# Layer 1's attention heads: the last two chunks of the value weighing move into the next head, with two accumulator banks

## The reference

```python
q = (hidden_states @ Wq.T + bq) * scaling          # 128 x 256, 16 heads of 16
k = key_value_states @ Wk.T + bk                   # 12544 x 256
v = key_value_states @ Wv.T + bv
scores = jnp.einsum('bhtd,bhsd->bhts', q, k) + bias
probs = jax.nn.softmax(scores, axis=-1)
attn = jnp.einsum('bhts,bhsd->bhtd', probs, v)
...
return attn @ Wo.T + bo
```

## Time and profile before

| | |
|---|---|
| median of 3 runs | 3257.34 us (3256.66, 3257.34, 3260.52) |
| profiled execution | 3260.9 us, its span 3259.2 us |
| mean granted TensorE clock | 0.968 |
| PE matmul busy | 3022.2 us (93%) |
| DVE busy | 1473.0 us (45%) |
| ACT busy | 1469.7 us (45%) |
| DMA, whole span | 577.84 MB, mean 177 GB/s |

### The profile page before, as it was taken

The page is one execution under the profiler, slowest core; times in us unless marked ns, Lnnn a source line. Parts: engine busy times, 40 slices in busy tenths (PEclk is TensorE's granted clock), DMA queues, the critical chain, the costliest instruction groups (busy, mean ns, idle before and its releaser), DMA issues. The chain is left out here.

```text
span 3259.2 us, 65496 instructions
## 1 busy us (share of the span) xinstructions
PE 3022.2 (93%) x23319; PEld 1909.9 (59%) x23319; DVE 1473.0 (45%) x4096; ACT 1469.7 (45%) x2522; POOL 230.1 (7%) x177
## 2 busy tenths in 40 slices
PE   8999999998797999998799999999999988999988
PEld 5555555556484666664455555555555675666678
DVE  3223232321526777765333333333333325888632
ACT  2332333333314788883244444444444432565621
POOL 2332313130000000000000000000000000000000
PEclk9999999999897999998999999999999987999979
DMA  6878787878249999965311111111111255656455
GB/s 222 285 259 255 252 253 253 253 241 277 96 144 365 363 363 373 359 258 188 136 40 59 40 59 40 59 59 40 59 55 44 78 167 152 153 148 154 117 185 188
DMA packets 301309, 577.84 MB, mean 177 GB/s; under 512 B 75569, under 2 KB 247425, under 8 KB 289921
## 3 DMA queue, kind: packets, MB, share of 16 engines
q1 hardware_dynamic: 301209, 576.58, 52.6%
HBM read 395.49 MB, written 181.05 MB: 177 GB/s over the span
## 5 line engine op out<-in xcount | busy, mean ns | idle before, releaser
L1762 DVE TENSOR_SCALAR_CACHE_REDUCE all_S<-l2x_scores 128x448 f32<-128x448 f32 x448 | 261.0, 620 | 413.9 <-PE l2x_scores L1678 413.9
L1826 ACT COPY early_nat_in<-l2x_key_bank 128x448 f32<-128x448 f32 x224 | 119.2, 532 | 485.1 <-PE l2x_key_bank L1665 483.7
L1665 PE MATMUL l2x_key_bank<-ahead_ctx,early_nat_out 128*64 128x448 f32 x1536 | 331.0, 552 | 0.0
L648 PE MATMUL prep_work<-prep_wv,prep_ctxT 128*128 128x512 f32 x688 | 300.3, 594 | 0.1
L1034 DVE CUSTOM_DVE_ANT_0 all_S<-l1x_scores,l1x_bias 128x448 f32<-128x448 f32 x448 | 261.7, 621 | 79.3 <-PE l1x_scores L946 70.4
L1270 DVE TENSOR_REDUCE l3x_rowmax<-l3x_scores 128x1 f32<-128x448 f32 x448 | 263.6, 622 | 39.5 <-PE l3x_scores L1190 38.0
L1345 ACT ACTIVATE l3x_pT<-l3x_turned 128x896 f32<-128x896 f32 x224 | 204.9, 917 | 164.4 <-PE l3x_turned L1198 161.3
L1701 PEld LDWEIGHTS l2x_out<-l2x_pT,l2x_v_half 128*64 128x64 f32 x3136 | 203.4, 137 | 96.8 <-issue 96.6
L1101 ACT ACTIVATE all_S<-all_S,l1x_negmax 128x896 f32<-128x896 f32 x224 | 232.8, 1042 | 50.4 <-DVE l1x_negmax L1047 34.5
L1841 ACT ACTIVATE all_S<-all_S,l2x_negmax 128x896 f32<-128x896 f32 x224 | 233.6, 1044 | 25.2 <-DVE l2x_total L1780 23.8
L1678 PE MATMUL l2x_scores<-early_nat_in,early_nat_out 64*128 64x448 f32 x896 | 229.1, 588 | 8.9 <-ACT early_nat_in L1826 8.2
(11 more groups left out here) (650 smaller groups left out, 4151.4 us busy)
## 6 DMA issues: line engine op xcount, KB each, us to landing
l1x_bias<-in_fside_Bx16xSxS_dram SPq DMA_DIRECT2D x112, 896.0 KB, 6.8
scratch_k<-prep_kparts SPq DMA_DIRECT2D x84, 672.0 KB, 3.3
l1x_k_half<-scratch_k SPq DMA_DIRECT2D x32, 1568.0 KB, 9.9
l2x_v_half<-scratch_v SPq DMA_DIRECT2D x32, 1568.0 KB, 6.3
keys_k<-scratch_k SPq DMA_DIRECT2D x32, 1176.0 KB, 7.3
scratch_k<-prep_kparts SPq DMA_DIRECT2D x56, 448.0 KB, 4.9
scratch_v<-prep_st_v SPq DMA_DIRECT2D x11, 2048.0 KB, 9.3
scratch_v<-prep_st_v SPq DMA_DIRECT2D x14, 1536.0 KB, 7.2
```

The lines of the kernel that those rows point to most:

```text
L648: last = nc.tensor.matmul(w[:, h, :], ctxT[:, k, j * P:(j + 1) * P], wv2[:, k, h * 512:(h + 1) * 512], start=(k == 0), stop=(k == KT - 1))
L1665: last = nc.tensor.matmul(keys_ps[half * VW:(half + 1) * VW, 0:HB], wk_cur[:, k, :], ahead.piece[c // 2][:, k, cols], start=(k == 0), stop ...
L1762: nc.vector.tensor_scalar(com.S[:, b * HB:(b + 1) * HB], scores_ps[half][:, 0:HB], 1.0, -3.4e38, ALU.mult, ALU.max, accum_out=rowmax[:, b: ...
```

## The change

`head_stream` is split: it keeps the one head of L0, in the same sequence, and a new `head_stream_biased` takes L1's sixteen. In it

- PE weighs chunks 9, 10 and 11 behind the last scores (chunk 8 still beside them). Chunks 12 and 13 are weighed in chunks 0 and 1 of the next head, behind its scores; `sum_tiles` follows in chunk 3. The last head weighs all its own.
- two accumulator banks take turns by the head's parity: the old `out` bank and `last_ps`, the bank that the projections use before and after. The product of `sum_tiles` goes beside the accumulators in the same bank. A head's first weighing waits for the division two heads back.
- DVE does `sum_of` at the head's end; `leave_bank` (copy of the bank, reciprocal) behind the scores of chunk 2 of the next head and `divide` behind those of chunk 4.
- PE's and DVE's loops have seven turns of two heads; heads 0 and 15 are written out.
- SP loads the second half of a head's values behind bias 1 of the head's own stretch and the first half of the next head's behind bias 5.
- DVE clears two banks at the start, behind a wait for `q_ready`.

```diff
-    def tensor_head(pe, h, following):
-        for c in range(GRP + lag):
-            if c < GRP:
-                turn(pe, h, c)
-                if following:
-                    scores(pe, h + 1, c)
+    def tensor_head(pe, h, odd, first=False, following=True):
+        for c in range(GRP):
+            turn(pe, h, c)
+            if following:
+                scores(pe, h + 1, c)
             if c >= lag:
-                weigh(pe, h, c - lag)
-        if tiles > 1:
-            sum_tiles(pe, h)
+                weigh(pe, h, odd, c - lag)
+            elif c < left and not first:
+                weigh(pe, h - 1, 1 - odd, GRP - left + c)
+            if c == left + 1 and not first:
+                sum_tiles(pe, h - 1, 1 - odd)
+        for c in range(GRP - lag, GRP - left if following else GRP):
+            weigh(pe, h, odd, c)
...
+        tensor_head(pe, 0, 0, first=True)
+        with pe.Fori(0, HEADS // 2 - 1) as i:
+            tensor_head(pe, i * 2 + 1, 1)
+            tensor_head(pe, i * 2 + 2, 0)
+        tensor_head(pe, HEADS - 1, 1, following=False)
+        sum_tiles(pe, HEADS - 1, 1)
...
+    def sum_of(dve, h):
         dve.wait_ge(exp_done, h * GRP + GRP)
         nc.vector.reduce_sum(total[:, :], rowsum[:, :], AX).then_inc(rowsum_taken, 1)
+
+    def leave_bank(dve, h, odd):
+        dve.wait_ge(weighed, h * GRP + GRP + ring)
+        nc.vector.tensor_copy(out_parts[:, :], banks[odd][:, 0:P]).then_inc(parts_ready, 1)
         dve.wait_ge(rowsum_taken, h + 2)
         nc.vector.reciprocal(inverse[:, :], total[:, :]).then_inc(out_step, 1)
+
+    def divide(dve, h, odd):
         dve.wait_ge(out_step, h + 1)
-        dve.wait_ge(weighed, h * GRP + GRP + ring)
...
+        dve.wait_ge(summed, h + 1)
+        nc.vector.tensor_scalar(att[:, bass.ds(h * VW, VW)], banks[odd][:, P:P + VW], inverse[:, 0:1], None,
                                 ALU.mult).then_inc(out_taken, 1)
...
-    def vector_head(dve, h, following):
+    def vector_head(dve, h, odd, first=False, following=True):
         for c in range(GRP):
             if by[c] == "v":
                 copy_turned(dve, nc.vector.tensor_copy, h, c)
             if following:
                 take_scores(dve, h + 1, c)
+            if c == left and not first:
+                leave_bank(dve, h - 1, 1 - odd)
+            if c == left + 2 and not first:
+                divide(dve, h - 1, 1 - odd)
         if following:
             max_of(dve, h + 1)
-        leave(dve, h)
+        sum_of(dve, h)
...
+                if i == 1 and second_of is not None:
+                    load_values(second_of, 1, first)
+                if i == 5 and first_of is not None:
+                    load_values(first_of, 0, first)
```

More of the change, by code:

```diff
@@ L860, in head_stream @@
     copied = {"v": S("copied_by_vector"), "s": S("copied_by_scalar")}
-    k_loaded = [S(f"k_loaded{j}") for j in range(2)]
-    v_loaded = [S(f"v_loaded{j}") for j in range(2 if heads > 1 else GRP)]
-    held, held_by_vector = S("held"), S("held_by_vector")
+    v_loaded = [S(f"v_loaded{c}") for c in range(GRP)]
     by = ["v" if c in by_vector else "s" for c in range(GRP)]
-    n_by = {e: by.count(e) for e in "vs"}
     rank = [by[:c + 1].count(by[c]) for c in range(GRP)]
-    more_scores = scores_ps is not None
     class Run:
@@ L872, in head_stream, with on_sync @@
     run = Run()
[L873 to L879, removed]
+    run.out_taken = out_taken
+    def on_sync(sp):
+        for c in range(GRP):
+            j, at = c // (GRP // 2), c % (GRP // 2)
+            sp.dma_start(v_half[j][:, at * GC:(at + 1) * GC, :], v_src(c)).then_inc(v_loaded[c], 16)
@@ new lines, in turn, with weigh @@
+    def turn(pe, c):
+        pe.wait_ge(exp_done, c + 1)
+        if c >= 2:
+            pe.wait_ge(copied[by[c - 2]], rank[c - 2])
+        for i in range(GC):
+            last = nc.tensor.transpose(turned_ps[c % 2][:, i * P:(i + 1) * P],
+                                       com.S[:, (c * GC + i) * P:(c * GC + i + 1) * P], com.ident[:, :])
+        last.then_inc(turned, 1)
+    def weigh(pe, c):
+        pe.wait_ge(v_loaded[c], 16)
+        pe.wait_ge(copied[by[c]], rank[c])
+        for i in range(GC):
+            k = c * GC + i
+            last = nc.tensor.matmul(out_ps[:, 0:vw], pT[c % ring][:, i * P:(i + 1) * P],
+                                    v_half[k // (CH // 2)][:, k % (CH // 2), :], start=(k == 0), stop=(k == CH - 1))
+        last.then_inc(weighed, 1)
@@ new lines, in on_tensor, with copy_turned, on_vector @@
+    def on_tensor(pe):
+        for c in range(GRP + lag):
+            if c < GRP:
+                turn(pe, c)
+            if c >= lag:
+                weigh(pe, c - lag)
+    def copy_turned(eng, copy, c):
+        eng.wait_ge(turned, c + 1)
+        if c >= ring:
+            eng.wait_ge(weighed, c - ring + 1)
+        copy(pT[c % ring][:, :], turned_ps[c % 2][:, 0:GW]).then_inc(copied[by[c]], 1)
+    def on_vector(dve):
+        nc.vector.reduce_max(negmax[:, :], com.mx0[:, :], AX).then_inc(max_step, 1)
+        dve.wait_ge(max_step, 1)
+        nc.vector.tensor_scalar(negmax[:, :], negmax[:, :], -1.0, None, ALU.mult).then_inc(negmax_ready, 1)
+        for c in range(GRP):
+            if by[c] == "v":
+                copy_turned(dve, nc.vector.tensor_copy, c)
+        dve.wait_ge(exp_done, GRP)
+        nc.vector.reduce_sum(total[:, :], rowsum[:, :], AX).then_inc(rowsum_taken, 1)
+        dve.wait_ge(rowsum_taken, 1)
+        nc.vector.reciprocal(inverse[:, :], total[:, :]).then_inc(out_step, 1)
+        dve.wait_ge(out_step, 1)
+        dve.wait_ge(weighed, GRP)
+        nc.vector.tensor_scalar(att[:, :], out_ps[:, 0:vw], inverse[:, 0:1], None, ALU.mult).then_inc(out_taken, 1)
@@ new lines, in on_scalar @@
+    def on_scalar(act):
+        act.wait_ge(negmax_ready, 1)
+        for c in range(GRP + 2):
+            if c < GRP:
+                s = com.S[:, c * GW:(c + 1) * GW]
+                nc.scalar.activation(s, s, ACT.Exp, bias=negmax[:, 0:1], scale=1.0,
+                                     accum_out=rowsum[:, c:c + 1]).then_inc(exp_done, 1)
+            if c >= 2 and by[c - 2] == "s":
+                copy_turned(act, nc.scalar.copy, c - 2)
+    run.on_sync, run.on_tensor, run.on_vector, run.on_scalar = on_sync, on_tensor, on_vector, on_scalar
@@ L891, in load_bias @@
             sp.dma_start(bias_tile[i][:, :], bias(h, i)).then_inc(bias_loaded[i], 16)
[L893 to L908, removed]
+        def load_values(h, j, first):
+            if not first:
+                hold(sp, held, weighed, (h - 1) * GRP + GRP // 2 * (j + 1) + ring)
+            sp.dma_start(v_half[j][:, :, :], v_src(h, j)).then_inc(v_loaded[j], 16)
+        def load_head(h, first=False, second_of=None, first_of=None):
+            for i in range(GRP // 2):
+                load_bias(h, i, first)
@@ L923, in on_sync @@
         sp.sem_inc(rowsum_taken, 1)
-        sp.sem_inc(out_taken, 1)
+        sp.sem_inc(out_taken, 2)
         for e in "vs":
             sp.sem_inc(copied[e], n_by[e])
[L927 to L935, removed]
+        load_head(0, first=True, first_of=0)
+        load_values(0, 1, True)
+        load_head(1)
+        load_head(2, first_of=1)
+        with sp.Fori(1, HEADS - 2) as h:
+            load_head(h + 2, second_of=h, first_of=h + 1)
+        load_values(HEADS - 2, 1, False)
+        load_values(HEADS - 1, 0, False)
+        load_values(HEADS - 1, 1, False)
     def scores(pe, h, c):
-        if k_loads is not None and c % (GRP // 2) == 0:
-            j = c // (GRP // 2)
-            pe.wait_ge(k_loaded[j], (h + 1) * 16 * n_k)
+        if c % (GRP // 2) == 0:
+            pe.wait_ge(k_loaded[c // (GRP // 2)], (h + 1) * 16)
         for b in (2 * c, 2 * c + 1):
[L943 to L952, removed]
+            pe.wait_ge(scores_taken, h * NB + b + 1)
+            j, at = b // GRP, b % GRP
+            nc.tensor.matmul(scores_ps[b % 2][:, 0:HB], q[:, bass.ds(h * P, P)],
+                             k_half[j][:, at * HB:(at + 1) * HB], start=True, stop=True).then_inc(scores_full, 1)
     def turn(pe, h, c):
@@ L974, in weigh @@
             k = c * GC + i
[L975 to L983, removed]
+            at = k % tiles * (P // tiles)
@@ L1002, in on_tensor @@
[L1002 to L1015, removed]
+        nc.tensor.matmul(banks[odd][:, P:P + VW], out_parts[:, :], select[:, :], start=True, stop=True).then_inc(summed, 1)
@@ L1018, in copy_turned, with on_tensor @@
+    def on_tensor(pe):
+        pe.wait_ge(cleared, 1)
+        for c in range(GRP):
+            scores(pe, 0, c)
+        tensor_head(pe, 0, 0, first=True)
[4 more added lines that the diff above has]
+        sum_tiles(pe, HEADS - 1, 1)
     def copy_turned(eng, copy, h, c):
@@ L1024, in take_scores @@
     def take_scores(dve, h, c):
-        if bias is not None and c % 2 == 0:
+        if c % 2 == 0:
             dve.wait_ge(bias_loaded[c // 2], h * 16 + 16)
         for b in (2 * c, 2 * c + 1):
```

(12 more changed lines are left out.)

143 lines of the change are left out of this document (76 added, 67 removed).

## The result

| | before | changed |
|---|---|---|
| median of 13 runs | 3256.66 us (3254.86 to 3264.68) | 3263.25 us (3261.0 to 3268.76) |
| ratio | | 1.0018, 95% interval 1.0011 to 1.0025 |
| profiled execution, its span | 3260.9, 3259.2 us | 3263.25, 3261.5 us |
| zero to zero, plain head | 28.53 us | 28.93 us |
| zero of head 1 to zero of head 15 | 401.98 us | 410.37 us |

The change made the kernel slower by 0.18%, which is 5.9 us of 3256.66; the two medians themselves lie 6.6 us (0.20%) apart. The effect is small beside the range of the runs, but the interval leaves out 1. "Zero" is the start of a head's exponential 0, as in the prediction.

What follows compares the result with a forecast made beforehand. No engine is full, so the order of waits bounds the kernel: PE up to chunk 2's scores, then DVE. 11 x 0.41 + 3 x 0.79 = 6.9 us, added to the median 3257.34, gives 3264.2; range 3256 to 3271.

Steps and rivals of the forecast that it cites:

- turn 0 behind zero: Start of PE's turn for chunk 0 after ACT's exponential 0: from 2.03 to 1.26 us, 0.77 gained.
- turn 2: Start of PE's turn for chunk 2, after two chunks with a weighing at 1.84 us each: 4.94 behind zero, against 4.83.
- additions on DVE: Bank copy and reciprocal between DVE's bank b5 and its copy of chunk 3: 0.30 us, high end 0.52.
- turn 5: Start of PE's turn for chunk 5, from which PE sets a steady pace: 10.10 us behind zero against 9.69, +0.41.
- tail, turn 5 to zero: From PE's turn for chunk 5 to the next head's exponential 0: 18.84 us, not touched by the change.
- table head's turn 5, later by: Heads 4, 8 and 12, where ACT loads its table: no gain at turn 0, so 9.31 becomes 10.10, +0.79 us.
- rival A: DVE's additions and the weighings are hidden, ACT's copies decide: turn 5 at 9.31, -4.2 us, 3253.1; chance 0.10.
- DMA share: The DMA engines' 0.91 share by stretch would fall because a longer head lowers it; priced at nothing.
- Rival B: Weighings in the next head cost only their back-to-back price: +1.6 us, 3258.9, a wash; chance 0.16.
- the 1.84 us rows: PE's profile rows of turn, scores, weighing, next turn: the forecast's price of a chunk with a weighing, 1.84 us.
- Rival D: The gain doesn't come, turn 0 stays at 2.03: 11 x 0.77 us more, 3272.7; chance 0.05.
- Rival C: DVE's doubled loop body is fetched anew at each of its 7 turns: 4.2 us more, 3268.4; chance 0.07.

Runs made afterwards that it cites:

- e2: Changed kernel with DVE's bank copy and reciprocal behind chunk 4's scores, PE's sum at chunk 7, the division behind chunk 8's; 3260.49 us against 3258.39 before.
- e1: Changed kernel with no weighing moved; bank copy, sum and division still in the next head, behind chunks 0, 1, 2; 3254.09 us against 3258.39 before.
- e4: Changed kernel with no weighing moved and the bank copy at the head's end; only PE's sum and DVE's division in the next head; 3254.18 us against 3258.39 before.
- e5: Changed kernel with the bank copied twice, first into a tile nobody reads; one run, plain head 29.13 us against 28.93 in the changed kernel.
- e3: e2's edit of the changed kernel, with the two weighings beside chunks 2 and 3 instead of 0 and 1; 3257.86 us against 3258.39 before.
- e6: Changed kernel with the values loaded in the old places of SP's queue; one run, plain head 28.93 us, as in the changed kernel.
- e7: Changed kernel with ACT's sixteen heads written out, one table load instead of four; 3260.15 us against 3258.06 before, ratio 1.0010.
- e8: Changed kernel with e4's and e7's edits together; 3251.10 us against 3258.06 before, ratio 0.9979.

## Why the prediction was right

Its steps, with what the rows show:

| step | forecast | measured |
|---|---|---|
| turn 0 behind zero | 1.26 | 1.26 to 1.27 |
| turn 2 | 4.94 | 4.95 |
| bank copy on DVE | 7.37 | 7.41 |
| additions on DVE | 0.30 us | 0.27 us |
| turn 5 | 10.10 | 10.09 |
| tail, turn 5 to zero | 18.84, unchanged | 18.83 to 18.84 |
| plain head, longer by | 0.41 | 0.40 |
| table head's turn 5, later by | 0.79 | 0.78 |
| heads 1 to 14, sum | 6.9 us | 8.4; 6.8 without head 12's clock |
| time | 3264.2, 6.9 above before | 3263.25, 6.6 above a before of 3256.66 (5.9 by the ratio) |

The mechanism is shown by experiment, not only by the agreement. With DVE's additions off their place turn 5 falls by 0.26 (e2), with the weighings gone as well by 0.52 more, to the 9.31 that rival A read from the table heads (e1, e4), and a doubled copy adds its 0.20 (e5). The other order, the weighings gone and the additions in place, was not run. The rows of e1 and e4 suggest that the additions would then cost next to nothing: DVE has 0.30 us of idle time in that place (e4), the additions took 0.27, and in e1 the division stands there with 0.22 us while turn 5 is at 9.31. So, by this estimate, the weighings alone release nearly all of the 0.78, though the additions alone release 0.26.

That the sum came so close owes something to errors that cancel. It took 0.41 for each of eleven heads and 0.79 for three. In the traces head 1 pays 0.64 and the heads behind a table head (5, 9, 13) 0.48, the other plain heads 0.36 to 0.40, and the table heads 0.68 to 0.71 without the clock's part: before, they took 18.91 to 18.93 us from turn 5 to the next zero, and not 18.84. And the 8.4 us of the profiled heads and the 6.6 of the medians differ by more than any of these. The forecast also had the DMA share fall from 0.91; it rose to 0.93 while the rate fell (366 to 360 GB/s). Nothing hung on that, since the tail stayed at 18.84.

Rival A was refuted as a forecast, but its number was right as the best case: e1 and e4 reach 9.31, and are 4.3 and 4.2 us faster than before by the medians (4.0 and 4.1 in the 14 heads). Rival B fell with turn 2 at 4.95; the 1.84 us rows priced a chunk with a weighing, the back-to-back ones did not. Rival D fell with turn 0. Rival C fell too: DVE's first bank comes 0.54 to 0.55 us behind PE's first scores in the odd heads, where a turn of its loop begins, and between 1130 and 1470 us all packets of the changed kernel are on the data queue. (Ahead of that, from 1047 to 1130 us, eleven packets are on instruction queues, against three before; the first turn of the two-head loops lies there, and its heads are 28.93 and 28.92 us long like the rest.)

```profile
DMA packets 18320, 110.78 MB, mean 326 GB/s; under 512 B 2496, under 2 KB 3264, under 8 KB 15632
## 3 DMA queue, kind: packets, MB, share of 16 engines
q1 hardware_dynamic: 18320, 110.78, 85.6%
```

So DVE's body of two heads is not fetched again at its turns. By the Trainium skill (Runtime: NRT & Kernel Launch, "Instruction fetch mechanics") a taken branch whose target the engine does not hold stalls until that is fetched. No such stall shows here, which agrees if the body fits in what the engine holds; how long the body is wasn't counted.

What the prediction missed is a term of its sum: it took nothing for the clock. In a table head the changed kernel leaves PE idle for 2.3 us (0.68 before), and in head 12 it was granted 1.2 GHz for a while behind it, which cost 1.57 us. How much of this is in the 13 timed runs isn't known. The slowdown came out on the line of 0.2% about which the forecast had split its odds (0.18% by the ratio, 0.20% by the medians), so the result favours neither part.

## What to carry to other kernels

Ask first which wait ends a stretch, and whether the work that is moved was inside it: here six weighings at a head's end filled PE's wait for the exponential almost exactly, and two of them were moved into the one stretch where PE and DVE feed each other without slack. What gained came from moving PE's sum and DVE's division out of the head's end to places where their engine waits (e4, with the copy left at the end; e1, with the copy moved too), not from moving products. Whether that needs a second bank was not tested: in e4 the division starts at 1200.72 and the first weighing of the same head at 1201.15, so one bank might have been free in time. When an edit ties an engine to another's start, whatever delays that start is paid in full from then on: a table load made a head 1.27 us longer in the changed kernel (30.20 for 28.93), while three of them cost the kernel before 2.6 us.

## What the runs showed of the hardware

- Behind 2.3 us of idle time of PE in a stream that is otherwise busy, the granted clock fell to the lower level in 6 of 15 cases (head 4, 8 or 12 of the changed kernel, e2, e3, e5 and e6; one profiled execution each), each worth 1.1 to 1.6 us. It fell behind 1.39 us (e1, e4) in none of 6, behind the 1.04 us of plain heads (the same five kernels and e7) in none, and behind 0.68 us (before) in none of 3.
- ACT's program of sixteen heads in one piece was fetched as it ran: queue q14 has 5 packets between 1120 and 1460 us of e8, and none there in e4, whose ACT loop holds four heads (on q8 it is 2 and 1). It cost nothing that the timeline shows: plain heads take 28.14 to 28.15 us in both.

```profile
q8 instruction: 2, 0.03, 0.0%
q14 instruction: 5, 0.04, 0.0%
```
